# Moving a transpose and its copy past the second up product in a hand-ordered Fourier layer and MLP kernel

## What is computed

```python
xn = layernorm(x)                       # over the 64 channels
xf = rfft2(xn)
o1 = relu(complex_product(xf, w1) + b1)
o2 = complex_product(o1, w2) + b2
o2 = o2 * ((|o2.re| > 0.01) | (|o2.im| > 0.01))
x  = x + irfft2(o2)
h  = gelu(layernorm(x) @ mw1 + mb1)     # 64 -> 256
x  = x + h @ mw2 + mb2                  # 256 -> 64
```

## Time and profile before

| | |
|---|---|
| median of 3 executions | 3589.64 us (3588.06 to 3591.62) |
| the profiled execution | 3587.65 us, its span 3585.8 us |
| mean granted TensorE clock | 0.968 of full speed |
| PE busy | 3274.0 us (91%) |
| DVE busy | 2395.3 us (67%) |
| ACT busy | 2337.6 us (65%) |
| POOL busy | 1657.7 us (46%) |

### The profile page before, as it was taken

The page is one execution under the profiler, slowest core; times in us unless marked ns, Lnnn a source line. Parts: engine busy times, 40 slices in busy tenths (PEclk is TensorE's granted clock), DMA queues, the critical chain, the costliest instruction groups (busy, mean ns, idle before and its releaser), DMA issues. The chain is left out here.

```text
span 3585.8 us, 53022 instructions
## 1 busy us (share of the span) xinstructions
PE 3274.0 (91%) x18286; PEld 1970.8 (55%) x18286; DVE 2395.3 (67%) x4150; ACT 2337.6 (65%) x3749; POOL 1657.7 (46%) x1389
## 2 busy tenths in 40 slices
PE   6936699999999999998999999999999999979689
PEld 2735364746464646464646464646464646334257
DVE  4956676767666776766666767676767664636667
ACT  3955576767676767677777666666666666646468
POOL 4445545464645455555454555545454543210242
PEclk9968899999999999999999999999999999989789
DMA  9850001010101011313120111111111111167898
GB/s 327 275 177 24 30 30 65 30 65 30 65 30 65 30 65 36 118 48 136 48 89 30 65 39 63 42 54 42 53 42 53 42 54 42 65 230 221 264 300 240
DMA packets 250272, 334.15 MB, mean 93 GB/s; under 512 B 21400, under 2 KB 194840, under 8 KB 241832
## 3 DMA queue, kind: packets, MB, share of 16 engines
q1 hardware_dynamic: 241584, 315.34, 26.0%
q0 software_dynamic: 7904, 15.57, 1.5%
q10 hardware_dynamic: 536, 0.03, 0.0%
HBM read 188.13 MB, written 142.74 MB: 92 GB/s over the span
## 5 line engine op out<-in xcount | busy, mean ns | idle before, releaser
L1528 ACT ACTIVATE a_hidden<-a_wide,a_up_b 128x1024 f32<-128x1024 f32 x512 | 568.5, 1110 | 137.2 <-PE a_wide L1710 135.8
L1710 PE MATMUL a_wide<-a_yc,a_up_fold 64*128 64x512 f32 x2048 | 579.9, 641 | 37.0 <-ACT a_hidden L1528 36.3
L1290 POOL TENSOR_TENSOR a_y<-a_o,a_mag 128x256 f32<-128x256 f32 (+1 forms) x512 | 365.2, 738 | 388.4 <-DVE a_mag L1392 388.4
L1721 PE MATMUL a_result<-a_hidden,a_down 128*64 128x512 f32 x2048 | 495.9, 604 | 32.5 <-DVE a_x L1403 32.3
L1248 POOL TENSOR_TENSOR a_y<-a_x,a_stat 128x512 f32<-128x512 f32 x256 | 267.8, 1047 | 520.1 <-DVEq L1437 503.0
L1375 DVE TENSOR_TENSOR a_o<-a_bank,a_mix_b 128x512 f32<-128x512 f32 (+1 forms) x272 | 181.5, 667 | 275.5 <-PE a_bank L1667 271.7
L1685 PEld LDWEIGHTS a_bank<-a_dft_h,a_g 128*128 128x128 f32 x2080 | 272.4, 191 | 128.9 <-issue 128.9
L1667 PEld LDWEIGHTS a_bank<-a_mix,a_o 128*128 128x128 f32 x2080 | 253.6, 192 | 152.8 <-issue 131.3
L1667 PE MATMUL a_bank<-a_mix,a_o 128*128 128x128 f32 x2080 | 299.1, 286 | 8.2 <-DVE a_o L1375 4.2
L1721 PEld LDWEIGHTS a_result<-a_hidden,a_down 128*64 128x64 f32 x2048 | 128.0, 136 | 314.1 <-issue 291.1
L1422 DVE TENSOR_REDUCE a_stat<-a_sq 128x16 f32<-128x1024 f32 x240 | 290.6, 1211 | 9.2 <-ACT a_sq L1562 8.2
(11 more groups left out here) (209 smaller groups left out, 6228.0 us busy)
## 6 DMA issues: line engine op xcount, KB each, us to landing
rows<-a_x SPq DMA_DIRECT2D x112, 512.0 KB, 2.7
a_x<-rows SPq DMA_DIRECT2D x105, 512.0 KB, 4.2
box_xc<-in_x SPq DMA_DIRECT2D x16, 1024.0 KB, 16.5
box_x<-in_x SPq DMA_DIRECT2D x64, 256.0 KB, 4.4
turned<-box_o SPq DMA_DIRECT2D x64, 256.0 KB, 3.8
a_y<-turned SPq DMA_DIRECT2D x16, 1024.0 KB, 11.9
box_x<-rows SPq DMA_DIRECT2D x16, 1024.0 KB, 25.9
planes<-box_work SPq DMA_DIRECT2D x64, 256.0 KB, 3.6
```

Of the source, the lines that this page charges most:

```text
L1290: ins = G.tensor_tensor(y[n % 2][:, :, to].rearrange("p c k -> p k c"), o2[:, j % 3, lo:4, r], mask[:, lo:4], ALU.mult)
L1528: A(hidden[:, i % 2, j], wide[:], ACT.Gelu, bias=up_b2[:, l, j:j + 1]).then_inc(s_hid, 1)
L1710: mm = M(wide[:, half * BANK:(half + 1) * BANK], up_fold[cs, l, j * P:(j + 1) * P], yc[cs, i % 2], start=True, stop=True)
L1721: mm = M(result[half * C:(half + 1) * C, :], down[:, l, j, :], hidden[:, i % 2, j, half * BANK:(half + 1) * BANK], start=j == 0, stop=j == ...
```

## The change

In each period PE's `turn(Q + 1)` moves from ahead of slot 1 to behind `mlp_up(Q, 1)`, ahead of slot 2. On ACT `operand(Q + 1)` moves from ahead of the magnitudes of slot 0 to behind `gelu(Q, 1)`. No instruction is added or removed.

```diff
 @block.scalar
                     parts(n, q, 0, inverse, forward, spectrum, backward)
-                    if 0 <= Q + 1 < BLOCKS * RUNS:
-                        operand(Q + 1)
                     parts(n, q, 0, other, other, magnitude, other)
...
                     if mlp:
                         gelu(Q, 1)
+                    if 0 <= Q + 1 < BLOCKS * RUNS:
+                        operand(Q + 1)
 @block.tensor
                     if 0 <= Q - 2 < BLOCKS * RUNS:
                         turn_back(Q - 2)
-                    if 0 <= Q + 1 < BLOCKS * RUNS:
-                        turn(Q + 1)
                     if q == BACKWARD_SLOT // 4:
                         parts(n, q, 0, inverse, forward, spectrum, backward)
                     parts(n, q, 1, inverse, forward, spectrum, backward)
                     if mlp:
                         mlp_up(Q, 1)
+                    if 0 <= Q + 1 < BLOCKS * RUNS:
+                        turn(Q + 1)
                     parts(n, q, 2, inverse, forward, spectrum, backward)
```

## The result

The changed kernel takes 3626.35 us in the median of 4 executions (3620.99 to 3628.75), the kernel before 3588.85 (3587.0 to 3591.62, 4 executions of the same series): a ratio of 1.0103 with a 95% interval of 1.0091 to 1.0115. It is slower by 37.5 us, about 1%. Run again later beside other kernels it took 3622.0 (5 executions, ratio 1.0091, 1.0078 to 1.0105). The forecast was 3617, range 3600 to 3632.

The account below looks back on a forecast made before the run. PE, 91% busy, and its own order were taken to set the time. +1.2 us a round over 14 rounds (17), 2.3 in round 14 and 8.5 in the last made 28 us: 3617 us forecast, range 3600 to 3632.

Parts of the forecast that it names:

- The pattern of the plain period: MLP-only periods (q = 3, last round): turn leaves the first GELU's shadow; period 5.97 in place of 5.36, +0.6 us.
- The switch of tiling modes: Turn between up and down products: two mode switches for one; drain estimate 0.05 us, edge rows about 0.16, turn taken as 0.6.
- q = 1 and 2, and 13 to 15: Two groups of periods in each round, forecast at +0.25 us together and +0.17 us together.
- the copy, 0.6, and 0.15 to PE: End of q = 2: after square and GELU, copy and handover delay the next up product, 1320.24 in place of 1319.99.
- q = 4: Turn's 1.07 us wait for POOL vanishes: gain 1.35 and a little in the forward part behind it, −1.4 us.
- The premise that the distances hardly differ from round to round: Whole kernel: instruction distances hardly vary between rounds, so one round of 176.4 us was worked through period by period.
- q = 6, 10 and 12: Three periods of each round, forecast at +0.25, +0.6 and +0.16 us.
- q = 5, 7 to 9 and 11: Periods with PE back to back and both slots full: turn costs 0.44 us at either place, so 0.
- The last round: Pure MLP periods: all 16 but q = 4 and the last lose 0.6 us each, 8.5 us together.
- Rival 1: Faster: moved turn falls into waits the down product already has, only gains remain, 27 us, 3563; chance 0.07.
- Rival 2: No change: earlier DVE and ACT chains give back losses in q = 0, 3 and 10 (1.8), 3590; chance 0.09.
- Rival 3: ACT takes over: copy delays the next up product by 0.6 in three more periods a round, 3642; chance 0.08.

Follow-up runs that it names:

- e3: Kernel before, with the first GELU of each step treating only 128 of its 1024 columns (timing only): 3577.42 us, one execution.
- e4: Changed kernel, with the first GELU of each step treating only 128 of its 1024 columns (timing only): 3585.46 us, one execution.
- e2: Kernel before with only ACT's copy moved as in the change, PE's turn left in its old place: 3596.03 us, ratio 1.0021.
- e11: Changed kernel, with DVE making q = 4's two layernorm sums ahead of the first inverse addition: 3612.74 us, one execution.
- e12: Kernel before; turn, copy ahead of second up product, GELU in q = 4, 13; in q = 4 DVE sums earlier, POOL's normalise behind slot 1's subtraction: 3563.84 us.
- e6: Kernel before, with turn moved behind slot 1 but ahead of the second up product, copy ahead of the second GELU, in q = 4 alone: 3587.02 us.
- e10: Kernel before, with only DVE's two layernorm sums in q = 4 made ahead of the first inverse addition: 3586.64 us, ratio 0.9992.
- e8: The changed kernel run again, unaltered, for its interval and a second profile: 3622.0 us.
- e1: Kernel before with only PE's turn moved as in the change, ACT's copy left in its old place: 4064.12 us, ratio 1.1327.

## Why the prediction was right, point by point

*The pattern of the plain period* was right to 0.02: second up product at 2.44 of 2.43, turn at 3.50 of 3.49, down at 4.08 of 4.1, PE's wait 0.72 of 0.8. e3 and e4 show that it is the shadow of the GELU that was left, and that the two edges cost 0.19 where I took 0.16.

*The switch of tiling modes.* That a switch drains the array is a rule of the Trainium skill ("TensorEngine Tiling (Array Packing)", "Key Properties"). No run shows a drain as such, but the sign agrees: with the GELU out of the way the place with one more switch is dearer by 0.19 (e4 less e3). The 0.05 that I had estimated from the drain of about 128 cycles in the Trainium skill ("TensorE: Matmul & The Clock Gate", "What happens when you issue a matmul") is too small for it: the extra is 0.15 in q = 12 and 13 and 0.19 in the last round.

*q = 1 and 2, and 13 to 15* were each about 0.2 too dear. The step that failed is "the copy, 0.6, and 0.15 to PE": e2 shows that putting the copy in adds 0.4. (The numbers in that sentence add up to 1320.32, not 1320.24; both are too late.) In q = 2 that hides the new wait: q = 3 was to start with a wait for the copy and has none. At the start of q = 0 the new wait is there, as predicted, for 0.37:

```profile
1305.01 1.10 ACT L1528 ACTIVATE a_hidden<-a_wide,a_up_b 128x1024 f32<-128x1024 f32 x1
1306.01 0.59 ACT L1534 ACTIVATE a_yc<-a_turned 128x512 f32<-128x512 f32 x1
...
1306.65 0.70 PE L1710 MATMUL a_wide<-a_yc,a_up_fold 64*128 64x512 f32 x2 [0.37 <-ACT a_yc L1534]
```

*q = 4* was the largest miss: −0.74 for −1.4 in the median, 8.1 us when the 14 rounds are added up. "And a little in the forward behind it" was the wrong sign: the down product does start 1.35 earlier in the period, as predicted, but the forward part then waits for the inverse additions. I had followed PE's and POOL's lists through q = 4 and not the DMA ahead of DVE's addition. In the changed kernel:

```profile
1332.71 3.12 SPq L1169 DMA_DIRECT2D a_x<-rows  x2
1339.05 0.69 DVE L1344 TENSOR_TENSOR a_x<-a_bank,a_x 128x512 f32<-128x512 f32 x1 [2.26 <-DMA a_x<-rows]
...
1342.94 2.05 PE L1656 MATMUL a_bank<-a_dft_w,a_y 128*128 128x128 f32 x16
...
1344.55 0.69 DVE L1349 TENSOR_TENSOR a_x<-a_bank,a_x 128x512 f32<-128x512 f32 x1
1345.29 2.05 PE L1656 MATMUL a_bank<-a_dft_w,a_y 128*128 128x128 f32 x16 [0.30 <-DVE a_x L1349]
```

e11 and e12 confirm it: once that chain is short, q = 4 gives 1.27 and 1.35.

*The premise that the distances hardly differ from round to round* was too strong. In rounds 0, 7 and 8 q = 2 lasts 5.50 in the kernel before, 0.14 over the plain 5.36, so the turn finds no wait to fall into; in rounds 0 and 7 q = 1 and 2 lose 1.0 together where I had 0.25.

*q = 6, 10 and 12* came out as worked out, to 0.01. In q = 10 slot 1's product waits 0.34 for ACT where the turn had stood. *q = 5, 7 to 9 and 11*, forecast at 0, are 0.3 a round shorter together. In q = 5, 7, 8 and 9 it is 0.04 each, and the timeline of q = 8 shows where: the product behind the up product took 0.99 to the next group and takes 0.90 behind the turn, while the turn takes 0.49 in place of 0.44. It is the exchange of edges that I had counted in q = 4 alone. For the 0.13 in q = 11 no run isolates the cause.

*The last round* cost 7.9 of 8.5: its q = 7 gained the wait that the turn had there for POOL.

*Rival 1* (faster) fell as argued: the down product's waits for DVE did take in the turn in q = 2, 14 and 15, nowhere else. *Rival 2* (no change) fell: q = 0, 3 and 10 lose 1.78, and the chains give back 0.04 in q = 13 to 15. *Rival 3* (ACT takes over) fell: waits for the copy make 5.1 us.

*The total.* The sum was 28; 32.4 was measured in the MLP periods. Against the forecast, q = 4 makes 8.1 more and q = 0 and 1 of round 8 make 3.4 more, nearly all of it the clock. q = 13 to 15 make 3.4 less and the periods forecast at 0 make 3.1 less; the rest, 0.6 less, is spread. So errors of 11.5 and 7.1 us stand against each other, and that the total is off by 4.4 only is in part luck. The pattern of the plain periods, which carries most of the sum, isn't. Two small slips are in the working: round 14 adds up to 2.4 and not 2.3, and there are 76 exposed places and not 72, since those of round 14 in q = 0, 3, 10 and 12 were left out. Between the medians the kernels lie 37.5 us apart, 33.5 in the later series.

## What to carry to other kernels

Where an engine waits for another at a fixed point, work placed ahead of that point is free up to the length of the wait, and costs its full time behind it if that engine sets the time there: compare start to start with and without the piece before moving it. An edit that takes a wait away gains only as far as the next chain that ends there allows, so follow each input of the instruction behind it, the DMA and the third engine too; q = 4 needed three edits, to the turn and its copy, to DVE's sums and to POOL's `normalise`. The first alone (e6) and the second alone (e10) showed nothing; the third alone wasn't run. A copy behind a GELU on ScalarE costs less than its duration, here 0.4 for 0.6.

## What the runs showed of the hardware that I had not expected

Single stretches of a lower granted clock turn up inside the MLP periods. Periods q = 0 and 1 of round n = 8 take 10.98 and 10.77 us in the changed kernel, with a granted clock of 0.84: about a third of each at 1.2 GHz, the lower of the two levels. In the second profile of it (e8) the same two periods have it again, 10.99 and 10.76 at 0.84, and q = 0 and 1 of n = 7 join them, 10.98 and 10.74. First the changed kernel's two rows in the table of stretches:

```profile
1851.07:1862.05 10.98, 8.80 (x30) 3.21 (x28) 5.29 (x5) 7.07 (x8) 3.47 (x2) 0.84 0.41 143
1862.05:1872.82 10.77, 8.73 (x29) 3.03 (x29) 7.77 (x18) 6.78 (x7) 4.57 (x3) 0.84 0.24 97
```

In the kernel before the same two periods take 8.61 each at full clock:

```profile
1837.44:1846.05 8.61, 7.06 (x30) 2.65 (x28) 5.38 (x5) 6.83 (x8) 3.73 (x2) 1.00 0.53 187
1846.05:1854.66 8.61, 7.02 (x31) 2.67 (x30) 6.91 (x16) 6.62 (x7) 4.58 (x3) 1.00 0.30 122
```

e11 tells the two parts of the difference apart. It has the order of the changed kernel on PE and ACT, and the same two periods take 9.40 and 9.16 there, at full clock. So of the 2.4 and 2.2 the order makes 0.8 and 0.6, and the clock 1.6 in each.

What brings the clock down isn't shown. In the changed kernel PE idles 1.74 us for `mlp_delta` in q = 0 of n = 8 before it falls; e11 has such waits too (up to 1.7) and no fall in these periods. Nor does it take the change: in the kernel before, q = 4 of n = 6 has a granted clock of 0.89 over its 15.98 us. In e1, where PE waits 81 times for o1's copy, up to 2.7 us and 164.5 in all, the granted clock is down to 0.96 over all the MLP periods together. Two more such stretches in e8 make 3.2 us, and its profiled execution is 1.6 longer than the first one's, 3622.59 for 3620.99. What makes the rest of the spread of the changed kernel (up to 3628.75) the profiles don't tell.
